# Shared values of two heads weighed at once in three passes, and a second transposition moved behind the queries

## The reference

```
x = layernorm(hidden)
q = rope(x @ w_q)                    # 32 heads of 128
k, v = rope(x @ w_k), x @ w_v        # 8 heads, each shared by 4 query heads
lq = x @ w_lq                        # 128 latent numbers per token
lk, lv = rope(lq @ w_lk), x @ w_lv   # 32 heads of 128, one for each query head
attn = causal_attention(q, k, v)     # with the shared keys and values
lat  = causal_attention(q, lk, lv)   # the same queries with their own keys and values
hidden = hidden + attn @ w_o + lat @ w_lo
```

## Time and profile before

| | us |
|---|---|
| median of 3 runs | 1802.27 |
| lowest and highest | 1800.79, 1804.77 |
| the profiled execution: time | 1804.75 |
| its span, first to last instruction | 1802.9 |
| TensorE busy in it | 1742.7 |
| VectorE, ScalarE, GpSimd busy | 1095.0, 1083.6, 931.1 |

### The profile page before, as it was taken

One profiled execution on the slowest core, in us unless ns is written; L12 is line 12 of the kernel. 1 busy time (PEld: TensorE's weight loads), 2 busy tenths in 40 slices (PEclk: granted clock), 3 DMA queues, 4 the chain that ended last, 5 costly groups with the idle time before them and its releaser, 6 DMA issues.

```text
span 1802.9 us, 32176 instructions
## 1 busy us (share of the span) xinstructions
PE 1742.7 (97%) x11116; PEld 1520.7 (84%) x11116; DVE 1095.0 (61%) x3305; ACT 1083.6 (60%) x3077; POOL 931.1 (52%) x1170
## 2 busy tenths in 40 slices
PE   7999999999999999999999999999999998899798
PEld 6789999999999998999899899989888776677567
DVE  6675465556456546645654664565566677788756
ACT  3355566567556656655765664566563264788864
POOL 4555545455544555554555554455542255777850
PEclk9999999999999999999999999999999999999999
DMA  4300021012002101200110120020012121000101
GB/s 145 109 27 7 18 60 36 1 43 64 7 18 59 36 1 48 65 1 19 59 36 1 49 64 1 19 75 21 1 59 59 42 60 46 2 2 2 37 12 47
DMA packets 35424, 65.79 MB, mean 36 GB/s; under 512 B 4032, under 2 KB 4672, under 8 KB 35264
## 3 DMA queue, kind: packets, MB, share of 16 engines
q1 hardware_dynamic: 35264, 63.73, 11.7%
HBM read 61.62 MB, written 2.10 MB: 35 GB/s over the span
## 4 chain that ended last, share of the span: by engine, by line
PE 76%; DVE 8%; ACT 8%; issue 5%; POOL 3%; DMA 0%; SPq 0%; DVEq 0%; POOLq 0%; ACTq 0%
PE bank L363 58%; PE bank L1105 6%; PE bank L1092 4%; PE bank L1107 3%; ACT s L1217 2%; PE bank L1672 2%; PE bank L1643 1%; ACT s L1738 1%; DVE h L761 1%; PE bank L1659 1%; DVE work L772 1%; POOL h L839 1%; DVE work L1319 1%; ACT h L684 1%; POOL rstd L328 1%
## 5 line engine op out<-in xcount | busy, mean ns | idle before, releaser
L363 PE MATMUL bank<-W,oT 128*128 128x512 f32 x1632 | 432.2, 400 | 0.6 <-DVE x L1875 0.6
L1425 POOL TENSOR_TENSOR qk<-work,qk 128x512 fp32r<-128x512 f32 (+1 forms) x160 | 193.9, 1212 | 427.0 <-ACT qk L1208 427.0
L363 PEld LDWEIGHTS bank<-W,oT 128*128 128x128 f32 x1632 | 288.3, 189 | 48.5 <-DVE x L1875 1.1
L1224 ACT COPY pt<-bank 128x384 f32<-128x384 f32 x256 | 122.0, 477 | 324.0 <-PE bank L1092 323.3
L1417 POOL TENSOR_TENSOR work<-work,table 128x512 f32<-128x512 f32 (+1 forms) x160 | 190.8, 1192 | 132.8 <-ACT work L1203 132.8
L1217 ACT ACTIVATE s<-s,neg_max 128x128 f32<-128x128 f32 (+1 forms) x512 | 227.5, 445 | 49.1 <-DVE neg_max L1333 48.1
L363 PE MATMUL bank<-W,xnA 128*128 128x320 f32 (+1 forms) x1056 | 191.0, 335 | 2.3 <-DVE xnA L348 1.7
L1310 DVE TENSOR_TENSOR work<-bank,table 128x512 f32<-128x512 f32 (+1 forms) x160 | 102.1, 638 | 130.0 <-ACT work L1203 129.9
L363 PEld LDWEIGHTS bank<-W,xnA 128*128 128x128 f32 x1056 | 166.3, 189 | 15.2 <-DVE xnA L348 2.6
L1438 POOL TENSOR_TENSOR s<-s,inv_sum 128x256 f32<-128x256 f32 x256 | 168.2, 657 | 0.0
L363 PE MATMUL bank<-qk 128*128 128x256 f32 (+1 forms) x768 | 165.9, 351 | 0.9 <-POOL qk L1425 0.9
(11 more groups left out here) (111 smaller groups left out, 3501.8 us busy)
## 6 DMA issues: line engine op xcount, KB each, us to landing
raw<-in_weights SPq DMA_DIRECT2D x215, 256.0 KB, 2.7
x<-in_x SPq DMA_DIRECT2D x8, 256.0 KB, 5.4
out<-x SPq DMA_DIRECT2D x8, 256.0 KB, 2.1
row<-in_bias_rows SPq DMA_DIRECT2D x5, 256.0 KB, 2.7
table<-in_constants SPq DMA_DIRECT2D x4, 240.0 KB, 3.1
b_qk<-in_bias_rows SPq DMA_DIRECT2D x1, 512.0 KB, 3.5
b_val<-in_bias_rows SPq DMA_DIRECT2D x1, 256.0 KB, 3.0
table<-in_constants SPq DMA_DIRECT2D x1, 66.0 KB, 2.4
```

The costliest lines, as they stand in the source:

```text
L363: last = nc.tensor.matmul(out_ap, lhs(i), rhs(j), start=start and k == 0, stop=stop and k == 2)
L1224: nc.scalar.copy(pt0[:, k, :], bank[PT][:, 0:3 * P]).then_inc(a_pt, 1)
L1425: nc.gpsimd.tensor_tensor(lo, work[:, 2 + s, st.columns(what)], hi.bitcast(F32), ALU.subtract).then_inc(a_rope_lo, 1)
```

## The change

The shared values are the same for all four heads of a group. The change puts two heads' shared results into one bank, and computes them for both heads at once with `product`: the values are split into HI and LO (`vs`), and so are the turned shared probabilities of both heads (`pt_pair`), which takes a subtraction on VectorE in each step (`turned_lo`). `weigh_pair` runs in the steps with h 0 and h 2; in h 1 and h 3 no shared values are weighed, and `turn(1)` stands behind the queries. The own values are weighed as before, by float32. The rounding of the shared result is one 128x512 operation for a pair, and the output products of the shared results come one to three steps later than the heads: one in h 0, two in h 1, none in h 2, one in h 3. Chunk 13 is split in step 3 and no longer in 17, chunk 12 in 17 and no longer in 16. The values' second half is a rounding, a copy and a subtraction.

```diff
-SPLIT_AT = {2: [17, 14], 3: [18], 11: [1], 12: [0, 2], 13: [3, 6], 14: [4, 7], 15: [8, 9],
-            16: [10, 11, 15, 12], 17: [16, 13]}
+SPLIT_AT = {2: [17, 14], 3: [18, 13], 11: [1], 12: [0, 2], 13: [3, 6], 14: [4, 7], 15: [8, 9],
+            16: [10, 11, 15], 17: [16, 12]}
...
-WEIGHTS_FOR = {2 + h: [C_WO + h, C_WLO + h] for h in range(GH)}
+WEIGHTS_FOR = {2: [C_WLO], 3: [C_WO, C_WLO + 1], 4: [C_WO + 1, C_WLO + 2],
+               5: [C_WO + 2, C_WO + 3, C_WLO + 3]}
...
             def turn(k):
-                n, s = st.near(-1).inst(k)
+                n, s = before.inst(k)
                 pe.wait_ge(a_norm, n + 1)
-                pe.wait_ge(a_pt, n + 1)
+                if k == 0:
+                    pe.wait_ge(a_pt_own, before.number() + 1)
+                else:
+                    pe.wait_ge(a_pt_lo, before.number() + 1)
...
+            def weigh_pair():
+                pe.wait_ge(a_pt_lo, before.number() + 1)
+                pe.wait_ge(a_own_lo, before.number() + 1)
+                to = bank[OB][:, :].rearrange("p (e q) -> p e q", e=2)
+                product(to, lambda p: vs[p][:, 0, :],
+                        lambda p: pt_pair[p][:, :, 0:2, :].rearrange("p e b q -> p e (b q)"), True, False)
+                product(to[:, :, P:SEQ], lambda p: vs[p][:, 1, :],
+                        lambda p: pt_pair[p][:, :, 2, :], False, True).then_inc(a_pv_pair, 1)
+
+            def weigh_own():
+                col = before.h * P
+                if before.h == 0:
                     pe.wait_ge(a_proj_free, before.fill(3)[0] + 3)
-                pe.wait_ge(a_pt, n + 2)
-                pe.wait_ge(a_o_lo, n + 1)
+                pe.wait_ge(a_pt_own, before.number() + 2)
+                if before.paired():
+                    pe.wait_ge(a_pair_lo, before.pair() + 1)
+                else:
+                    pe.wait_ge(a_own_lo, before.number() + 1)
...
-            if lag1:
-                weigh(0)
+            if lag2 and st.h == 0:
+                output(0, st.near(-3))
+            if lag1 and before.paired():
+                weigh_pair()
                 turn(1)
             if st.queries and not st.first:
                 a0_queries(pe, st)
+            if lag1 and not before.paired():
+                turn(1)
...
-            if lag2:
-                output(0)
+            if lag2 and st.h in (1, 3):
+                output(0, st.near(-3))
+            if lag2 and st.h == 1:
+                output(0, st.near(-2))
+            if lag2 and st.h != 1:
+                output(1, st.near(-2))
             if lag1:
-                weigh(1)
-            if lag2:
-                output(1)
+                weigh_own()
+            if lag2 and st.h == 1:
+                output(1, st.near(-2))
...
             if lagging(st):
-                turned_out(0)
+                turned_hi()
...
+            if lagging(st) and before.paired():
+                pair_hi()
             if lagging(st):
-                result_hi(0)
-                turned_out(1)
+                turned_own()
...
             if lagging(st):
-                result_hi(1)
+                own_hi()
...
+            def turned_lo():
+                dve.wait_ge(a_pt_hi, before.number() + 1)
+                hi, lo = [pt_pair[i][:, before.h % 2, :, :].rearrange("p b q -> p (b q)") for i in (HI, LO)]
+                nc.vector.tensor_tensor(lo, bank[PT][:, 0:3 * P], hi.bitcast(F32),
+                                        ALU.subtract).then_inc(a_pt_lo, 1)
+
+            def pair_lo():
+                dve.wait_ge(a_pair_hi, before.pair() + 1)
+                hi, lo = [o_pair[i][:, :, :].rearrange("p e q -> p (e q)") for i in (HI, LO)]
+                nc.vector.tensor_tensor(lo, bank[OB][:, :], hi.bitcast(F32),
+                                        ALU.subtract).then_inc(a_pair_lo, 1)
...
-                nc.vector.tensor_copy(lvv[:, tt, half * HALF:(half + 1) * HALF],
-                                      bank[fs][:, 0:HALF]).then_inc(a_proj_free, 1)
+                if half == 0:
+                    nc.vector.tensor_copy(lvv[:, tt, 0:HALF], bank[fs][:, 0:HALF]).then_inc(a_proj_free, 1)
+                    return
+                own = GH * HD - HALF
+                shared = bank[fs][:, own:HALF]
+                nc.vector.tensor_copy(vs[HI][:, tt, :], shared).then_inc(a_v_hi, 1)
+                nc.vector.tensor_copy(lvv[:, tt, HALF:GH * HD], bank[fs][:, 0:own])
+                dve.wait_ge(a_v_hi, st.values_before() + tt + 1)
+                nc.vector.tensor_tensor(vs[LO][:, tt, :], shared, vs[HI][:, tt, :].bitcast(F32),
+                                        ALU.subtract).then_inc(a_proj_free, 1)
 
             turn_of = None if st.last_group else st.g
             if before.queries:
                 a0_rotate(dve, before, "q")
+            if lagging(st):
+                turned_lo()
             if st.heads:
                 minima(0)
                 minima(1)
...
-            if lagging(st):
-                result_lo(0)
+            if lagging(st) and before.paired():
+                pair_lo()
```

More of the change, by code:

```diff
@@ L934, in near, with values_before, paired, pair @@
                 return Step(self.g, self.s + d)
+            def values_before(self):
+                return 2 * (self.g * BATCH + self.batch)
+            def paired(self):
+                return self.s % 2 == 1
+            def pair(self):
+                return self.number() // 2
             def number(self):
@@ L1094, in turn, with output @@
                 last.then_inc(a_turned, 1)
[L1096 to L1100, removed]
-                    pe.wait_ge(a_proj_free, before.fill(3)[0] + 3)
-                pe.wait_ge(a_pt, n + 2)
-                pe.wait_ge(a_o_lo, n + 1)
-                nc.tensor.matmul(bank[OB][:, 0:SEQ], lvv[:, 0, col:col + P], pt0[:, k, 0:2 * P],
-                                 start=True, stop=False)
[L1107 to L1113, removed]
+            def weigh_pair():
[9 more added lines that the diff above has]
+                if before.h == 0:
+                    pe.wait_ge(a_proj_free, before.fill(3)[0] + 3)
+                pe.wait_ge(a_pt_own, before.number() + 2)
[3 more added lines that the diff above has]
+                    pe.wait_ge(a_own_lo, before.number() + 1)
+                nc.tensor.matmul(bank[OB][:, 0:SEQ], lvv[:, 0, col:col + P], pt_own[:, 0:2 * P],
+                                 start=True, stop=False)
+                nc.tensor.matmul(bank[OB][:, P:SEQ], lvv[:, 1, col:col + P], pt_own[:, 2 * P:3 * P],
+                                 start=False, stop=True).then_inc(a_pv_own, 1)
+            def output(k, done):
+                first, end = done.h == 0 and k == 1, done.h == GH - 1 and k == 1
                 if first:
@@ L1117, in output @@
                     pe.wait_ge(a_lq_lo, 2)
-                pe.wait_ge(a_o_lo, n + 2)
+                if k:
+                    pe.wait_ge(a_own_lo, done.number() + 2)
+                    of, slot = o_own, done.number() % 2
+                else:
+                    pe.wait_ge(a_pair_lo, done.pair() + 1)
+                    of, slot = o_pair, done.h % 2
                 w = ((C_WLO if k else C_WO) + done.h) * CH
                 for tt in range(2):
-                    last = product(bank[OUTB[tt]][:, :], lambda p: oT0[p][:, s, tt * P:(tt + 1) * P],
+                    last = product(bank[OUTB[tt]][:, :], lambda p: of[p][:, slot, tt * P:(tt + 1) * P],
                                    lambda p: W[p][:, w:w + CH], first, end)
@@ L1220, in exponentials, with turned_hi, turned_own, pair_hi @@
                 last.then_inc(a_exp, 1)
[L1222 to L1229, removed]
+            def turned_hi():
+                act.wait_ge(a_turned, before.inst(0)[0] + 1)
+                nc.scalar.copy(pt_pair[HI][:, before.h % 2, :, :].rearrange("p b q -> p (b q)"),
+                               bank[PT][:, 0:3 * P]).then_inc(a_pt_hi, 1)
+            def turned_own():
+                act.wait_ge(a_turned, before.inst(1)[0] + 1)
+                nc.scalar.copy(pt_own[:, :], bank[PT][:, 0:3 * P]).then_inc(a_pt_own, 1)
+            def pair_hi():
+                act.wait_ge(a_pv_pair, before.pair() + 1)
+                nc.scalar.copy(o_pair[HI][:, :, :].rearrange("p e q -> p (e q)"),
+                               bank[OB][:, :]).then_inc(a_pair_hi, 1)
+            def own_hi():
+                act.wait_ge(a_pv_own, before.number() + 1)
+                nc.scalar.copy(o_own[HI][:, before.number() % 2, :], bank[OB][:, 0:SEQ]).then_inc(a_own_hi, 1)
             turn_of = None if st.last_group else st.g
             if lagging(st):
-                turned_out(0)
+                turned_hi()
             if before.queries:
@@ L1381, in a0_vector_step @@
             if lagging(st):
-                result_lo(1)
+                own_lo()
             if st.h == 1 and not st.second:
```

38 lines of the change are left out of this document (24 added, 14 removed).

## The result

| | before | changed |
|---|---|---|
| median of 5 runs each, us | 1803.03 | 1810.21 |
| lowest and highest | 1800.79, 1804.77 | 1809.37, 1811.35 |
| span of the profiled execution | 1802.9 | 1808.4 |

The ratio is 1.0038, interval 1.0028 to 1.0049: 7 us slower, against the 10.5 us forecast. The time of 1812.8 was 2.6 us too high.

A forecast was written before the change was run, and what follows sets the result against it. TensorE, busy 97%, was taken as the bound, with the loop through the other engines within 0.2 us in split steps. Products -16.0, old waits -5.3, new waits +31.8: net +10.5, 1812.8 us; range 1799 to 1822.

The forecast's parts named there:

- Removed and added on TensorE: Each pair of heads loses 1.30 us of weighings and gets 1.05 of products: 16.0 us less in 64 pairs.
- The subtraction: VectorE's new 128x384 operation between rotation and minima in every step: 0.55 us, 0.47 to the next start.
- The loop: Minima, exponentials, copies, splits, swap, sine, rotation: 7.42 us beside TensorE's 7.59 with splits, 8.86 in step 14; the subtraction adds 0.47.
- The waits in the last batch: TensorE waits 0.16 in step 14, 1.17 in 15, 1.11 in 16: together 2.44 us, in 7 groups.
- The first batch of a group: Second transposition in step 3 waits 0.73, pair in step 4 waits 1.11: together 1.84 us, in 8 groups.
- Waits taken away, -5.3: Waits that steps 14 and 15 have now go away: 5.3 us, taken between 2.9 and 8.9.
- The new waits, +31.8: New TensorE waits in batches with splits: 7 x 2.44 + 8 x 1.84 = 31.8 us.
- Batches without splits: Loop shorter by 1.16 a step; the pair in h 0 is ready some 0.7 us before TensorE, no wait.
- The rival of spreading: Waits spread to 17 batches without splits, or last group's extra normalisation meets fuller VectorE: 1821, up to 1828; chance 0.13.
- The move of the second transposition, priced at nothing: In h 1 and 3, moving it behind the queries only exchanges neighbours: no cost if its operands are there.
- Weights, order of splits: Changed chunk order costs nothing; rival that weights come late, +20 us, chance 0.02.
- The loop covered after all: Rival: engines' lining up wrong by 2 us, so no new waits: 1781 us; chance 0.16.

The follow-up runs named there:

- e1: Changed kernel with VectorE's subtraction of the rounded shared probabilities put ahead of the query rotation: 1793.36 us, ratio to before 0.9946.
- e3: Changed kernel, weight splits cut to 32 of 512 columns from the second group on: 1784.93 us; kernel before with the same short splits: 1797.09 us.
- e6: Changed kernel with the second transposition put back ahead of the queries in h 1 and h 3: 1867.94 us, ratio to before 1.0354.
- e5: Kernel before with only the changed kernel's new order of weight splits: 1802.62 us, ratio to before 0.9996.
- e7: Changed kernel with the subtraction ahead of the query rotation and the weight splits spread, many behind the values: 1784.67 us, ratio to before 0.9895.
- e4: Changed kernel with VectorE's new subtraction done twice, first into a spare buffer: 1861.26 us, ratio to before 1.0323.

## Why the prediction was right, by its steps

- **Removed and added on TensorE.** Right. The six products of a pair start 1.05 before the next transposition (532.28 to 533.33), as summed from two neighbours. The gain was 16.0 by the forecast, 0.50 a batch; the unsplit batches give 0.57, 17.8 in all. The pairs are 0.51 of it (four weighings of 0.65 against two pairs of 1.05). The rest is the neighbours that I had priced at nothing: by distances of starts in one unsplit batch of each kernel, the queries take 0.18 less (1.43 in h 1 and h 3, where they now follow three-pass products), the output products 0.12 less, the own weighings 0.14 and the values 0.08 more.
- **The subtraction.** Right: 0.549 by its group, next start 0.47 behind (564.28 to 564.75). The Trainium skill (VectorE: DVE Perf Modes, "The DRAIN you can't avoid") would hold the next operation until the pipe is empty; here the minima start 0.08 before the subtraction's recorded end, so this trace doesn't agree. The same paragraph goes on that a next operation that is not held starts earlier, which the prediction passed over, and with that the trace does agree. The estimate of 525 ns from its table (same page, "The TRN2 errata") is 4% short of the measured 549. These are the groups by shape, 113 to 1360 us:

```profile
L1403 DVE TENSOR_TENSOR pt_pair<-bank,pt_pair 128x384 fp32r<-128x384 f32 x128 | 70.3, 549 | 0.0
L1409 DVE TENSOR_TENSOR o_pair<-bank,o_pair 128x512 fp32r<-128x512 f32 x64 | 44.0, 688 | 11.4 <-ACT o_pair L1280 11.4
L1280 ACT CAST o_pair<-bank 128x512 fp32r<-128x512 f32 x64 | 36.1, 564 | 2.3 <-PE bank L367 2.3
```

- **The loop.** Right, and the part that decides (e1 takes the subtraction out of it, e3 the splits). From one subtraction to the next it is 9.32 from step 14 to 15 (forecast 9.56) and 7.63 from 15 to 16 (forecast 7.64).
- **The waits in the last batch.** The pair in 16 waited 1.00 (forecast 1.11). The second transposition in 15 waited 0.44, not 1.17: VectorE came 0.4 sooner there (20.46 from the first transposition of 13 instead of 20.85), TensorE 0.3 later. Behind the 0.3 is a wait that I had left out: in 14 the own weighing waits 0.42 for the remainder of the pair's result, as it does in the kernel before. I had taken that wait away and it stayed. The pair in 14 didn't wait (forecast 0.16). Together 1.86, not 2.44; without the own weighing's, 1.44.
- **The first batch of a group.** The second transposition in 3 waited 0.37, not 0.73, the pair in 4 1.0 (forecast 1.11).
- **Waits taken away, -5.3.** Too much: the 0.42 of step 14 didn't go. Waits of that kind are 4.9 us after (L1141) where they were 8.9, so 4.0 went.
- **The new waits, +31.8.** The term that was mis-sized: by the waits it is 21.9, though 5.2 of that stand in the last group, which I had counted only for its first batch. The largest miss is the second transposition's, 0.4 where I had 1.17 and 0.73.
- **The sum.** By starts, as it was made, the products gave 17.8 and not 16.0, and all waits net were +23.1 (1.6 of it the clock) and not +26.5: together +5.3, half of the forecast's 10.5. The idle time of the page, +18.4, and its busy time, -12.9, are the same sum cut in another place. That the time on the median is off by 2.6 only is in part luck: the medians lie 7.2 apart where the profiled spans lie 5.5 apart, and the median before came out 0.8 higher than the one that I added to. I also gave batches with splits 1.3 us more than before; they took 0.7 and 0.8.
- **Batches without splits.** No wait, as said, with 0.52 to 0.60 us to spare in step 8 (forecast 0.7), but 0.16 in step 12, behind a split that I had not counted there. The rival of spreading was nearer than I gave it, and its other half came in small: in the last group, where it named the extra normalisation, the closing batch grew by 0.9.
- **The move of the second transposition, priced at nothing.** Nearly right as to the products (the neighbours together gain 0.07 a batch, above), and it makes nothing wait in the groups without full splits (e3). But the price holds for this direction only: with the transposition in its old place the kernel is 58 us slower (e6).
- **Weights, order of splits.** Hidden, as said (e5).
- **The loop covered after all** didn't happen. It is what the change would have been worth: e3, e7.

Opening and closing batches took 4.6 us; I had counted the first as one like the others and the last group for its first batch only. The opening batch grows by 2.5 (37.1 to 39.6), of which the lowered clock is 1.6; in e7, without that, it is 36.4. In four of e7's last batches (38.9) the own weighing of step 14 still waits 0.45; the other three are 38.6. Its other waits at that line, 2.0 of 3.8 us, stand in the opening batch and the last group. I tried nothing on them.

## What to carry to other kernels

Before giving a full engine's work to others, measure the loop through those others in each kind of step, not their busy share: a chain through VectorE, 64% busy, decided this change. What is added to such a loop goes where its engine already waits for another (here ahead of the rotation), and other work that can move, like the splits, goes beside the stretch that TensorE fills by itself. With its operations in another order, a change that loses 7 us here gains 18.

## What the runs showed of the hardware

The same operation costs a loop less than it is long: 0.47 for a recorded 0.55, and four of them 1.87 in a batch (e4). The granted clock was 0.991 to 0.996 of full speed over the span in all profiled executions, which hides stretches at half speed: one in the changed kernel's attention, in which 3.49 us of products take 5.06, and five in e6's. The two slowest, e6 and e4, have the lowest mean, 0.991 and 0.993, and TensorE's longest idle time, 126.9 and 115.1 us where the changed kernel has 78.6. Each of these stretches stands behind a wait of TensorE of 2.0 to 2.5 us; four other waits of that length in e6 and the 2.46 in e7 have none behind them.
